# Software gathers issued eight tiles ahead, the row transpose put in front of the down product, and three stage heads reordered

## The reference

```
# layer 0: 8 experts, hidden 512, gelu, biases        layer 1: 8 experts, hidden 256, silu(x w1) * (x w3)
weights = softmax(ln(t) @ gate)                       # [2048, 8]
top 2 experts of each token, with their weights
expert_out[t, e] = act(ln(t) @ w1[e] (+ b1)) @ w2[e] (+ b2)
t = t + sum over the token's 2 experts of weight * expert_out
```

## Time and profile before

| | |
|---|---|
| median of three runs | 657.54 us (657.32 to 657.60) |
| the profiled execution: its own time | 658.85 us |
| its span, first to last instruction | 657.0 us |
| busy: PE, DVE, POOL, ACT | 80%, 67%, 44%, 42% of the span |
| mean granted clock of TensorE, as a share of full speed | 0.767 |
| layer 0's expert loop, from its first up product to the last scatter's end | 200.35 to 317.55 us |
| layer 1's expert loop, the same | 530.88 to 637.72 us |

### The profile page before, as it was taken

One profiled execution on the slowest core, in us unless ns is written; L12 is line 12 of the kernel. 1 busy time (PEld: TensorE's weight loads), 2 busy tenths in 40 slices (PEclk: granted clock), 3 DMA queues, 4 the chain that ended last, 5 costly groups with the idle time before them and its releaser, 6 DMA issues. The chain is left out here.

```text
span 657.0 us, 10582 instructions
## 1 busy us (share of the span) xinstructions
PE 523.2 (80%) x3070; PEld 403.0 (61%) x3070; DVE 442.0 (67%) x1266; ACT 274.2 (42%) x714; POOL 291.7 (44%) x272
## 2 busy tenths in 40 slices
PE   9997967996589898999247999999856778777752
PEld 5784555976537787887135877777636445555531
DVE  2737579989783566443178799999996854445435
ACT  4613253102204444444114899999942023333321
POOL 1192457976434677665112111111111257777740
PEclk9797596998579999999655555555555798998995
DMA  5000060000901111111230000000004011111116
GB/s 214 1 0 1 13 243 0 1 2 9 311 8 34 45 45 43 48 45 37 63 82 0 1 2 0 0 0 0 1 2 128 1 36 49 49 52 45 51 37 189
DMA packets 26508, 31.07 MB, mean 47 GB/s; under 512 B 3105, under 2 KB 21538, under 8 KB 26338
## 3 DMA queue, kind: packets, MB, share of 16 engines
q1 hardware_dynamic: 21474, 20.29, 9.6%
q0 software_dynamic: 4992, 10.23, 6.0%
HBM read 20.16 MB, written 10.36 MB: 46 GB/s over the span
## 5 line engine op out<-in xcount | busy, mean ns | idle before, releaser
L1091 POOL DMA_INDIRECT rows_out<-yo,idy x78 | 80.7, 1035 | 55.7 <-DVE yo L1453 45.7
L1085 POOL DMA_INDIRECT xg<-rows_in,idx x78 | 75.8, 972 | 34.0 <-issue 21.9
L1445 DVE TENSOR_TENSOR hidden<-ps,hidden 128x512 fp32r<-128x512 f32 (+1 forms) x78 | 43.3, 555 | 51.9 <-ACT hidden L1154 51.9
L1147 ACT ACTIVATE hraw<-ps 128x512 f32<-128x512 f32 (+1 forms) x78 | 38.3, 491 | 83.9 <-PE ps L1249 83.9
L1270 PE MATMUL ps<-wHL,hidden 128*128 x234 | 69.8, 350 | 1.5 <-DVE yo L1453 0.4
L1140 ACT ACTIVATE xa<-ps 128x128 fp32r<-128x128 f32 x78 | 21.6, 278 | 87.9 <-PE ps L1235 87.8
L1273 PE MATMUL ps<-wHL,hidden 128*128 x234 | 54.4, 232 | 0.0
L1605 ACT ACTIVATE p<-s 128x256 bf16<-128x256 bf16 x128 | 51.6, 414 | 3.4 <-DVE s L1797 2.9
L1270 PEld LDWEIGHTS ps<-wHL,hidden 128*128 128x128 f32 x234 | 44.7, 191 | 9.8 <-issue 9.3
L1247 PE MATMUL ps<-wHL,xa 128*128 x78 | 35.1, 450 | 16.6 <-issue 13.4
L1440 DVE TENSOR_TENSOR hraw<-hraw,ps 128x256 f32<-128x256 f32 x39 | 16.4, 421 | 45.3 <-ACT hraw L1147 45.3
(11 more groups left out here) (286 smaller groups left out, 1398.4 us busy)
## 6 DMA issues: line engine op xcount, KB each, us to landing
wraw<-in_ex SPq DMA_DIRECT2D x2, 2048.0 KB, 10.0
rows_in<-both SPq DMA_DIRECT2D x8, 512.0 KB, 6.2
both<-rows_out SPq DMA_DIRECT2D x16, 256.0 KB, 5.1
wraw<-in_ex SPq DMA_DIRECT2D x1, 3072.0 KB, 12.5
w<-in_pack SPq DMA_DIRECT2D x1, 1582.0 KB, 8.4
xg<-rows_in,idx POOLq DMA_INDIRECT x78, 2.6
rows_out<-yo,idy POOLq DMA_INDIRECT x78, 2.3
xs<-in_x SPq DMA_DIRECT2D x4, 256.0 KB, 4.7
```

Source lines behind the costliest of these rows:

```text
L1085: pool.indirect_dma_start(xg[:, j % NXG, :], None, xs_d[:], bass.IndirectOffsetOnAxis(idx[:, j:j + 1], 0)).then_inc(ld[j % NXG], 16)
L1091: pool.indirect_dma_start(ys_d[:], bass.IndirectOffsetOnAxis(idy[:, j:j + 1], 0), yo[:, j % NYO, :], None).then_inc(st[j % NYO], 16)
L1147: act.activation(hraw[:, j % 2, :], ps[:, HB + j % 2, 0:hid], ACT.Gelu if layer == 0 else ACT.Silu).then_inc(z["act"], 1)
L1445: dve.tensor_tensor(hL[:, j % 2, :], ps[:, HTB + j % 2, 0:hid], hH[:, j % 2, :].bitcast(F32), ALU.subtract).then_inc(z["hL"], 1)
```

## The change

1. POOL issues eight gathers in front of its loop, and in the loop gather(j+8) behind scatter(j). The number of buffers stays at six, so gathers 6 and 7 wait for the transposes of tiles 0 and 1.
2. PE's order in step p becomes up(p), hidden_transposed(p-1), transposed(p+2), down(p-2).
3. The upper parts of layer 1's weights are copied by ACT, in the same steps 3 to 10, behind high(p+2).
4. DVE makes `lanes` by 32 instructions of 128 columns that compare against one number for each partition (now kept as float32), where it took 4 of 1024 columns that compare two tensors.
5. Layer 1's gate: PE transposes chunks 0 and 1 and makes their logits, and then does the same for chunks 2 and 3. Before it transposed all four first.
6. SP issues fetch(0) and fetch(1) at the end of layer 0's expert block instead of at the start of `block4`.
7. In `block4` DVE's first steps become combine(0), moments of 0, combine(1), pair_apply(0), moments of 1; before, the moments of 1 stood in front of pair_apply(0).

```diff
@@ -998,7 +998,7 @@
             idf, aside = own(f"idf_{layer}", [P, NT]), own(f"aside_{layer}", [P, NT])
             pos = own(f"pos_{layer}", [P, TOPK, R], I32)
             parts = own(f"parts_{layer}", [P, 2, R * TOPK], I32)
-            tile_of, lane_of = own(f"tile_of_{layer}", [P, R * TOPK], BF16), own(f"lane_of_{layer}", [P, R * TOPK], BF16)
+            tile_of, lane_of = own(f"tile_of_{layer}", [P, R * TOPK], BF16), own(f"lane_of_{layer}", [P, R * TOPK])
             wtmp = own("wtmp", [P, P]) if layer == 0 else None
             oh = own(f"oh_{layer}", [P, NT], F32R)
             xg = own(f"xg_{layer}", [P, NXG, P])
@@ -1033,9 +1033,9 @@
                             sp.dma_start(by_place(xs_d, k, s), xc[:, s]).then_inc(z["xst"], 16)
                 for n in range(NYO):
                     sp.wait_ge(st[n], st0[n] + 16 * len(range(n, NT, NYO)))
+                for c in range(NCH if layer == 1 else 2):
+                    fetch(sp, c)
                 if layer == 1:
-                    for c in range(NCH):
-                        fetch(sp, c)
                     for c in range(NCH):
                         sp.wait_ge(z["fo"], z0["fo"] + c + 1)
                         sp.dma_start(out.rearrange("b c n -> c b n")[:, 2 * c:2 * c + 2, :],
@@ -1103,13 +1103,13 @@
                     pool.wait_ge(s_zero, 16)
                 pool.wait_ge(z["xst"], z0["xst"] + 16 * S * TOPK)
                 pool.wait_ge(z["idx"], z0["idx"] + 1)
-                for j in range(NXG):
+                for j in range(NXG + 2):
                     gather(j)
                 pool.wait_ge(z["idy"], z0["idy"] + 1)
                 for j in range(NT):
                     scatter(j)
-                    if j + NXG < NT:
-                        gather(j + NXG)
+                    if j + NXG + 2 < NT:
+                        gather(j + NXG + 2)
 
             @blk.scalar
             def _(act):
@@ -1162,6 +1162,10 @@
                         hidden_high(p - 1)
                     if p + 2 < NT:
                         high(p + 2)
+                    if layer == 0 and 3 <= p < 3 + E:
+                        if p == 3:
+                            act.wait_ge(s_raw3, 16)
+                        act.activation(wHL3[:, p - 3, 0, :], wraw3[:, p - 3, 1, :], ACT.Copy).then_inc(s_h3, 1)
                 if layer == 1:
                     for c in range(NCH):
                         act.wait_ge(z["ftp"], z0["ftp"] + c + 1)
@@ -1185,14 +1189,14 @@
                         if s == 0:
                             ln_transposes(pe, nn, gs["ltp"], 1, 0, 4)
                 else:
-                    for c in range(NCH):
-                        pair_transposes(pe, c, c4)
-                    for c in range(NCH):
-                        pe.wait_ge(z["lt"], z0["lt"] + c + 1)
-                        for i in range(4):
-                            x = logits(row(1, i % 2, 2 * c + i // 2), pair_columns(c)[:, i * P:(i + 1) * P])
-                        if c % 2 == 1:
-                            x.then_inc(z["lgp"], 1)
+                    for half in ((0, 1), (2, 3)):
+                        for c in half:
+                            pair_transposes(pe, c, c4)
+                        for c in half:
+                            pe.wait_ge(z["lt"], z0["lt"] + c + 1)
+                            for i in range(4):
+                                x = logits(row(1, i % 2, 2 * c + i // 2), pair_columns(c)[:, i * P:(i + 1) * P])
+                        x.then_inc(z["lgp"], 1)
 
                 def ranks(g):
 
@@ -1281,10 +1285,10 @@
                         up(p)
                     if 1 <= p < NT + 1:
                         hidden_transposed(p - 1)
+                    if p + 2 < NT:
+                        transposed(p + 2)
                     if p >= 2:
                         down(p - 2)
-                    if p + 2 < NT:
-                        transposed(p + 2)
                 if layer == 1:
                     for c in range(NCH):
                         pe.wait_ge(z["fin"], z0["fin"] + c + 1)
@@ -1367,10 +1371,10 @@
                                               iotab[:, 0:NT][:, None].to_broadcast([P, RK, NT]), ALU.is_equal).then_inc(z["one"], 1)
                     dve.wait_ge(z["one"], z0["one"] + 1)
                     dve.tensor_scalar(rowno[:, :, 0], hits[:], wc("place"), None, ALU.mult)
-                    for q in range(CHK):
-                        some = slice(q * RK // CHK, (q + 1) * RK // CHK)
-                        dve.tensor_tensor(lanes[:, some], lane_of[:, some, None].to_broadcast([P, RK // CHK, P]),
-                                          iotab[:][:, None].to_broadcast([P, RK // CHK, P]), ALU.is_equal).then_inc(z["one"], 1)
+                    for i in range(RK):
+                        x = dve.tensor_scalar(lanes[:, i], iotab[:], lane_of[:, i:i + 1], None, ALU.is_equal)
+                        if i % (RK // CHK) == RK // CHK - 1:
+                            x.then_inc(z["one"], 1)
 
                 def tables():
 
@@ -1463,10 +1467,6 @@
                         result(p - 2)
                     if p + 2 < NT:
                         low(p + 2)
-                    if layer == 0 and 3 <= p < 3 + E:
-                        if p == 3:
-                            dve.wait_ge(s_raw3, 16)
-                        dve.tensor_copy(wHL3[:, p - 3, 0, :], wraw3[:, p - 3, 1, :]).then_inc(s_h3, 1)
                     if layer == 0 and 4 + E <= p < 4 + 2 * E:
                         e = p - 4 - E
                         dve.wait_ge(s_h3, e + 1)
@@ -1545,7 +1545,7 @@
 
         @block4.sync
         def _(sp):
-            for c in range(NCH):
+            for c in range(2, NCH):
                 fetch(sp, c)
 
         @block4.gpsimd
@@ -1838,15 +1838,20 @@
                 ln_moments(dve, chv, range(S), (2 * c, 2 * c + 1))
                 pair_variance(dve, chv, c, c4)
 
-            def summed(c):
-
-                combine(dve, 0, c)
+            def measured(c):
+
                 ln_moments(dve, chv, range(S), (2 * c, 2 * c + 1))
                 pair_variance(dve, chv, c)
 
+            def summed(c):
+
+                combine(dve, 0, c)
+                measured(c)
+
             summed(0)
-            summed(1)
+            combine(dve, 0, 1)
             pair_apply(dve, 0)
+            measured(1)
             pair_low(dve, 0)
             for n in range(4):
                 lower(*fragment(0, 0, n), bank=n)
```

More of the change, by code:

```diff
@@ L1839, in finished @@
                 pair_variance(dve, chv, c, c4)
+            def measured(c):
+                ln_moments(dve, chv, range(S), (2 * c, 2 * c + 1))
+                pair_variance(dve, chv, c)
             def summed(c):
                 combine(dve, 0, c)
-                ln_moments(dve, chv, range(S), (2 * c, 2 * c + 1))
-                pair_variance(dve, chv, c)
+                measured(c)
             summed(0)
-            summed(1)
+            combine(dve, 0, 1)
             pair_apply(dve, 0)
+            measured(1)
             pair_low(dve, 0)
```

## The result

The changed kernel takes 634.09 us (median of four runs, 633.17 to 636.38) where the kernel before takes 657.57 beside it: a ratio of 0.9646, with a 95% interval of 0.9619 to 0.9673. By the medians that is 23.5 us less. The profiled execution took 634.37 us, 24.5 less than the profiled one before (658.85). Its span is 632.6 us.

The account below looks back on a forecast made before the run. Layer 0's expert loop was taken as bound by a ring of waits, no engine full. Terms -11 - 7.8 - 5.1 - 0.5 + 0 = -24.4 us took the median from 657.54 to 633.1, range 627.5 to 641.

Parts of the forecast that it names:

- The lead: Both expert loops: gathers eight tiles ahead instead of six; in layer 0 about 5 us to spare before PE waits.
- the ring of scatter, gather, landing and transpose: Layer 0's expert loop: this chain of waits takes 5.17 us, longer than the two steps (5.12) that should cover it.
- PE's sum: Layer 0's loop end by PE: 35 steps of 2.56 us put up(38) at 295.45 instead of 310.05, or -14.6.
- the lengthened scatters: Layer 0's loop: seven scatters stay at 1427 ns against 990 while DVE writes lower weight parts, 3.1 us more.
- the margin: Layer 0's loop: 2 us kept back because POOL's and PE's paces are equal and a hiccup is not made up.
- The term, set at -11: Layer 0's expert loop: gain from earlier gathers and PE's new order, -11 us, between -8 and -14.6.
- POOL's sum: Loop end by POOL's scatters and gathers: layer 0's last scatter at 303.6 (-12.9), layer 1's at 628.4 (-8.4).
- The order: Both loops' tails: one down product now stands behind the last transpose, about 1.3 us in layer 0, 1.0 in layer 1.
- the slower rival: Both loops: landings pass 7.6 us, so transposes hold back down and scatter; at 8.3 us a total of 682; chance 0.03.
- The heads: Stage starts: barrier to combine(0) -3.8 us and pair_apply(0) -1.3, together -5.1; layer 1's first exponential -0.5.
- the gate: Layer 1's gate: first exponential at about 502.6 instead of 503.14, -0.5 us, between -1.4 and +0.3.
- Lanes: DVE, each layer: 32 instructions of 0.16 us, 5.1 against 4.8 undisturbed; forecast 0, ends -2.7 and +0.8.

Follow-up runs that it names:

- the lead alone: The kernel before with one change, gathers issued eight tiles ahead instead of six: 638.42 us, ratio 0.966.

## Why the prediction was right

**The lead.** The step that carried the forecast, the ring of scatter, gather, landing and transpose, held in each of its parts. With six ahead it sets the pace, with seven it stands at the engines' pace, with eight it is out of the way, and the lead alone gives the loops' whole gain. In layer 0 PE's pace decided, with 2.61 a step against the 2.56 of the undisturbed one, so up(38) came at 296.94 where PE's sum said 295.45: 1.5 us of small delays. POOL was ahead of its sum (gather(38) at 286.4, worked out as 288.4), because the lengthened scatters cost less than the 3.1 us set down: in before's trace five of DVE's eight subtractions of the lower parts (L1473) began ahead of a scatter and ran 0.5 us or more into it, in this one a single one did. The groups of POOL from 230 to 253 us, after, beside the earlier trace rows:

```profile
L1091 POOL DMA_INDIRECT rows_out<-yo,idy x9 | 9.8, 1094 | 2.7 <-issue 2.7
```

The step that was mis-sized is the margin: 2 us were taken off the smaller of the two sums (-12.9), while the delays came off the larger (-14.6). The term, set at -11, is -13.1. That POOL's sum gave nearly the last scatter's time (303.6 for 303.50) is luck, since PE's order decided. In layer 1 POOL's sum is the one that held: gather(38) came 78.3 us behind scatter(0) (78.1 worked out), its transpose 3.9 behind that (3.6) and the last scatter 9.5 behind the transpose (9.6). The term is -8.0 for -7.8.

**The order.** It was set down as one down product at each tail, 1.3 and 1.0 us. From the last transpose to the last scatter lie 10.3 and 9.5 us with it and 9.3 and 8.7 with it undone, so the tails cost 1.0 and 0.8. But undoing it moved the whole loops by +0.6 and -1.2, and the lead alone, also in the old order, agrees (104.9 and 97.9): in layer 0 PE's order and not the landing sets when the transpose comes, so it stands a down product earlier and the longer tail is no loss, while the steps are a little shorter (2.61 us, 2.63 in the old order); in layer 1, where the transpose follows its gather by 3.9 us, the tail is lost. That reading is argued from these rows; no run separates the two. That it could hold down back, the mechanism of the slower rival, is real; it needs the landing to be late, which the lead prevents.

**Edit 3.** Forecast 0, and undoing it changed nothing (633.77 beside 634.42). ACT's copies took 0.86 us each, where 0.84 was estimated, and the steps kept their 2.61.

**The heads.** Drain, fetch and moments came to -3.76 and -1.38, as forecast; the gate to -1.03 for -0.5, the exponential coming where the copies end, 0.5 us sooner than worked out.

**Lanes.** The price of one small instruction was right: (7.30 - 2.26) / 31 = 0.163 us each, forecast 0.16. The term failed in the last step: the 5.1 us were set equal to 4.8 and the difference dropped. As measured, `lanes` is 0.6 us longer in each layer. By the Trainium skill, "VectorE: DVE Perf Modes", section "The TRN2 errata — SBUF-src ops pay a fixed extra latency per instruction", many small tiles pay a latency each that one large tile pays once; the trace agrees in sign (7.30 and 6.75 us for 6.70 and 6.17).

**What was missed.** PE's spare products stand in no term of the prediction. They stand ahead of the first transpose, their length differs with the granted clock (4.93 us at 0.92, 7.06 at 0.63), and layer 1's start lost 1.8 us to them. The forecast total (-24.4) met the measured one (-24.5) because this and lanes, +2.4 together, with 0.5 behind the last scatter, stood against the 2.8 that the loops and the gate brought beyond their terms. So the terms hold one by one to within about 2 us, and that the total holds to 0.1 is luck. Why the products took 4.93 us in the one trace before stays open: the lead alone on the kernel before, with before's own head, has 6.90 there (one trace), so neither edit 4 nor edit 5 need be the cause.

## What to carry to other kernels

Where gathers are issued in turn with scatters that depend on the same chain, write the ring out: issue, landing, the consumer's place in its queue, result. Count how many tiles it closes over and compare with the engines' pace for that many; more lead helps until the ring is out of the way (here seven tiles came within 3.5 us of eight, and more than eight were not run), and an order that puts the waiting consumer ahead of what the ring needs shortens the ring's count and can cost far more than it gives. Before calling filler work free, look what stands behind it in the same queue.

## What the runs showed of the hardware

- Ten equal products of PE took between 4.5 and 7.4 us in these traces (4.53 at a granted clock of 1.00, 4.93 at 0.92, 7.06 at 0.63). Four of them in front of layer 0's loop, instead of ten, left the stretch from 200 to 205 us at 0.55 instead of 1.00, and the loop ended 1.2 us later. Two executions of the same changed kernel had 6.80 and 7.06, and 6.33 and 6.84 us; what decides it is not shown.
- A scatter of POOL grew only where a write of weights on DVE had begun ahead of it and ran well into it. The scatter takes 0.99 us by itself. In the trace before, two copies of 768 columns (L1469) began 0.16 and 0.17 us ahead of a scatter each, and these took 1.25 (the first lines below, for one). Of the eight two-input subtractions of the same size (L1473) five began ahead and ran 0.5 us or more into a scatter, and these scatters took 1.37 to 1.71; one began 0.27 us behind a scatter's start, and the scatter kept its 0.99. In the changed kernel, layer 0, one subtraction stretched a scatter to 1.47 (the second lines):

```profile
215.34 0.55 DVE L1469 CAST wHL<-wraw 128x768 fp32r<-128x768 f32 x1
215.50 1.25 POOL L1091 DMA_INDIRECT rows_out<-yo,idy  x1 [0.80 <-DVE yo L1453]
```

```profile
232.50 0.95 DVE L1473 TENSOR_TENSOR wHL<-wraw,wHL 128x768 fp32r<-128x768 f32 x1
232.84 1.47 POOL L1091 DMA_INDIRECT rows_out<-yo,idy  x1 [0.30 <-issue]
```

  The Trainium skill, "SBUF — State Buffer", section "SBUF: two separate sides", says that the ports which DVE and GpSimd share go for a whole instruction to whichever begins first, that a float32 copy within SBUF can take them, and that an operation with two SBUF inputs takes them only against a GpSimd operation that reads SBUF. These rows agree: both kinds stretched a scatter, and only where they began first. That it is these ports which the two wait for, no run separates. In the run in which DVE makes the copies again these lay over gathers that had begun before them (970 ns, unchanged), and took up to 0.72 us instead of 0.55 themselves.
